# A graph network on one core: receiver's term moved into the message, messages two chunks ahead, deviation in two halves

## The reference, cut to what matters

```python
h = relu(layernorm(x))
m = concat(h[dst], h[src]) @ W_pre.T + b_pre            # one message per edge
mx, mn, s1, s2 = segment max, min, sum(m), sum(m*m) over dst   # 0 where a node has no edge
mean = s1 / deg_c;  std = sqrt(relu(s2 / deg_c - mean * mean) + 1e-5)   # deg_c = max(degree, 1)
agg = concat(mx, mn, mean, std)
scaled = concat(agg, agg * log(deg_c + 1), agg / log(deg_c + 1))
x = x + (concat(h, scaled) @ W_post.T + b_post) @ W_lin.T + b_lin

h = relu(layernorm(x))
agg = segment_sum(edge_attr, dst) / max(degree, 1)
x = x + relu(concat(h, agg) @ W1 + b1) @ W2 + b2
```

## Time and profile before

| | |
|---|---|
| median of 3 runs | 1519.05 us |
| profiled execution, own time | 1520.14 us |
| its span, first to last instruction | 1518.3 us |
| PE busy | 1445.0 us (95%) |
| DVE busy | 1287.0 us (85%) |
| POOL busy | 1152.0 us (76%) |
| ACT busy | 1142.2 us (75%) |
| mean granted TensorE clock | 0.979 of full |

### The profile page before, as it was taken

How to read it: one execution, slowest core, us unless ns; L and a number is a source line. 1 busy time by engine, 2 the same in 40 slices (tenths; PEclk the granted TensorE clock), 3 DMA queues, 4 the chain that set the end, 5 groups by cost and what they waited for, 6 DMA issues and landing times.

```text
span 1518.3 us, 34851 instructions
## 1 busy us (share of the span) xinstructions
PE 1445.0 (95%) x8704; PEld 1246.4 (82%) x8704; DVE 1287.0 (85%) x4128; ACT 1142.2 (75%) x2760; POOL 1152.0 (76%) x1427
## 2 busy tenths in 40 slices
PE   2799999999999987999999999999999999999994
PEld 2698998998998976888888888888888888888883
DVE  4899999999999957888888888888888888888881
ACT  1699999999999965777777777777777777777772
POOL 0677777777877876788888888888888888888722
PEclk9699999999999998999999999999999999999997
DMA  3455555555555563343434434333333443444200
GB/s 80 153 204 200 208 200 200 212 198 203 209 196 209 204 228 104 116 116 116 119 111 114 116 113 113 115 114 116 116 115 115 117 117 116 117 119 119 91 16 13
DMA packets 166068, 210.91 MB, mean 139 GB/s; under 512 B 19710, under 2 KB 116217, under 8 KB 166026
## 3 DMA queue, kind: packets, MB, share of 16 engines
q1 hardware_dynamic: 144074, 162.88, 32.7%
q0 software_dynamic: 21952, 47.55, 10.5%
HBM read 123.96 MB, written 90.27 MB: 141 GB/s over the span
## 4 chain that ended last, share of the span: by engine, by line
PE 92%; DVE 2%; issue 2%; DMA 1%; POOL 1%; ACT 1%; SPq 1%; DVEq 0%; POOLq 0%
PE bank L573 12%; PE bank L614 8%; PE bank L617 7%; PE bank L611 7%; PE bank L608 7%; PE bank L607 7%; PE bank L582 6%; PE bank L711 6%; PE bank L699 5%; PE bank L674 3%; PE bank L592 3%; PE bank L594 3%; PE bank L593 3%; PE bank L556 3%; PE bank L564 3%
## 5 line engine op out<-in xcount | busy, mean ns | idle before, releaser
L464 POOL DMA_INDIRECT y<-nout,oidx x196 | 223.3, 1139 | 49.0 <-issue 46.0
L456 POOL DMA_INDIRECT rows<-table,idx x196 | 187.9, 958 | 59.7 <-issue 59.7
L607 PE MATMUL bank<-comb_lo,agg_hi 128*128 128x384 f32 x588 | 221.3, 376 | 0.8 <-ACT bank L885 0.8
L456 POOL DMA_INDIRECT hs<-table,idx x196 | 192.8, 984 | 29.4 <-issue 10.0
L385 POOL TENSOR_TENSOR runs<-nx,b_all 128x512 f32<-128x512 f32 x98 | 125.5, 1281 | 114.6 <-DVE nx L1081 114.6
L573 PE MATMUL bank<-w_sb,nut 128*128 128x128 f32 x1568 | 202.0, 282 | 1.5 <-ACT nut L806 1.5
L573 PEld LDWEIGHTS bank<-w_sb,nut 128*128 128x128 f32 x1568 | 183.9, 193 | 19.8 <-issue 10.0
L611 PE MATMUL bank<-comb_hi,agg_lo 128*128 128x384 f32 x588 | 198.2, 337 | 0.0
L608 PE MATMUL bank<-comb_hi,agg_hi 128*128 128x384 f32 x588 | 198.1, 337 | 0.0
L791 ACT ACTIVATE nh<-nx,nms,nrs 128x128 f32<-128x128 f32 x392 | 161.8, 483 | 1.1 <-DVE nms L1054 0.5
L614 PE MATMUL bank<-comb_sd,agg_sd 128*128 128x384 f32 x392 | 158.1, 485 | 0.0
(11 more groups left out here) (184 smaller groups left out, 4192.1 us busy)
## 6 DMA issues: line engine op xcount, KB each, us to landing
table<-rows SPq DMA_DIRECT2D x98, 512.0 KB, 2.7
rows<-in_x SPq DMA_DIRECT2D x98, 256.0 KB, 3.1
y<-nout SPq DMA_DIRECT2D x98, 256.0 KB, 2.7
inv<-inv_row SPq DMA_DIRECT2D x49, 256.0 KB, 5.0
keepm<-keepm_row SPq DMA_DIRECT2D x49, 256.0 KB, 5.8
attr<-in_edge_attr SPq DMA_DIRECT2D x48, 256.0 KB
keep<-keep_row SPq DMA_DIRECT2D x49, 128.0 KB, 3.6
reset<-reset_row SPq DMA_DIRECT2D x49, 128.0 KB, 4.6
```

The lines of the kernel that those rows point to most:

```text
L456: pool.indirect_dma_start(out=to[:, s, j, :], out_offset=None, in_=of, in_offset=bass.IndirectOffsetOnAxis(ap=idx[:, s, which, j:j + 1], a ...
L464: pool.indirect_dma_start(out=out, out_offset=bass.IndirectOffsetOnAxis(ap=oidx[:, c % 4, j:j + 1], axis=0), in_=eout[:, c % 2, j, :], in_ ...
L607: pe.matmul(acc[:, 0:SCALERS * P], hi, w_lo, start=False, stop=False, skip_group_check=True)
```

## The change

- **Message.** `sender_part` becomes `messages`: a second plain fp32 matmul adds the receiver's term (`wd_t`, `hdt`). `comb_h`, `hdl`, `receiver_low` and their three matmuls per tile in `layer0` go.
- **Table.** Its second half holds x1 of a node without edges (the first layer's result in the node passes) instead of x; the seed of the edge part is reduced by that node's constant. So the table store of chunk c leaves at SyncE's node step c instead of c-2 and waits for `n_x1`; x is loaded into a buffer of its own, and the norms wait for the table store of the chunk four before.
- **Two chunks ahead.** In step k, PE and ACT make the message of chunk k+2; DVE scans chunk k+1 as before, in another order.
- **Deviation.** It is split into `high_part` and `low_part` like the others; three fp32r matmuls replace the plain one.
- **POOL.** Its edge steps are written out (no loop), so that the index columns are read in place and the copies `idx` and `oidx` go; `copy_factors` moves to DVE. Small additions keep their place between the indirect DMAs.
- **Order.** DVE: `scan_attr(k)` moves from the head of the step to behind `mix(k, 1)` and the low part of the maximum. ACT: `scale_attr(k + 1)` moves from the middle to the head, in front of `squares(k - 1)` and `seed(k, 1)`. SyncE's `edge_step` is unchanged.

```diff
 # TensorE
-                for a in (MX, MN, ME):
+                for a in (MX, MN, ME, SD):
...
-                pe.matmul(acc[:, 0:SCALERS * P], agg_sd[:, c % 2, cols], comb_sd[:].rearrange("p s f -> p (s f)"),
-                          start=False, stop=False, skip_group_check=True)
-                for h, w in ((hdt, comb_h_lo), (hdl, comb_h_hi), (hdt, comb_h_hi)):
-                    mm = pe.matmul(acc[:, 0:SCALERS * P], h[:, c % 2, cols], w[:].rearrange("p s f -> p (s f)"),
...
-                pe.matmul(bank[3 + c % 2][:], ws_t[:], hst[:, c % 2, :], start=True, stop=True).then_inc(sem("e_b_psum"), 1)
+                pe.matmul(bank[3 + c % 2][:], ws_t[:], hst[:, c % 2, :], start=True, stop=False)
+                pe.wait_ge(sem("e_hdt"), c + 1 + EU * i)
+                pe.matmul(bank[3 + c % 2][:], wd_t[:], hdt[:, c % 2, :], start=False, stop=True).then_inc(sem("e_b_psum"), 1)
...
-                if ahead:
-                    turn_sender(k + 1, i)
-                    turn_receiver(k + 1, i)
                 if have:
                     turn_attr(k, i)
-                if ahead:
-                    sender_part(k + 1, i)
+                if edge(k + 2):
+                    turn_sender(k + 2, i)
+                    turn_receiver(k + 2, i)
                 if have:
-                    pe.wait_ge(sem("e_hdl"), k + 1 + EU * i)
                     layer0(k, 0, i)
                     layer0(k, 1, i)
+                if edge(k + 2):
+                    messages(k + 2, i)
                 if behind:
-                    turn_normed(k - 1, i, not ahead)
+                    turn_normed(k - 1, i, not edge(k + 2))
 # ScalarE, edge_step
                 if ahead:
-                    sender_turned(k + 1, i)
+                    scale_attr(k + 1, i)
+                if behind:
+                    squares(k - 1, i)
                 if have:
                     seed(k, 1, i)
                 if behind:
-                    squares(k - 1, i)
                     spread(k - 1, i)
-                if ahead:
-                    message_squared(k + 1, i)
+                if edge(k + 2):
+                    receiver_turned(k + 2, i)
+                    sender_turned(k + 2, i)
                 if behind:
                     normalise(k - 1, i)
                 if have:
                     seed(k, 2, i)
+                if ahead:
+                    mean_squared(k + 1, i)
                 if behind:
                     normed_turned(k - 1, i)
...
 # SyncE, node_step
-                c = k + 2
+                c = k
                 if node(c):
...
+                    sp.wait_ge(sem("n_x1"), c + 1 + NU * i)
 # GpSimd
-            run_passes(pool, node_step, edge_step)
+            run_passes(pool, node_step, edge_step, edge_loop=False)
```

More of the change, by code:

```diff
@@ L236, in run_passes @@
                 edge_step(k - N_HI + 1, 0)
+        if not edge_loop:
+            for k in range(0, E_HI):
+                edge_step(k, 0)
+            return
         for k in range(0, E_LOOP):
@@ L399, in node_step, with go, column, gather_tile @@
                     last.then_inc(sem("n_norm1_pool"), 1)
[L401 to L422, removed]
-                s = c % 4
-                pool.wait_ge(fixed, 1)
+            def go(n, c, name, count):
+                if name:
+                    pool.wait_ge(sem(name), count)
+                if c >= 1:
+                    pool.wait_ge(sem(f"e_paused{n}"), c)
+                pool.tensor_tensor(pause_go[:, n:n + 1], eps_col[:], eps_col[:], ALU.add).then_inc(sem(f"e_paused{n}"), 1)
+            def column(which, c, j):
+                return index[:, which, 2 * c + j // 2, j % 2:j % 2 + 1]
+            def gather_tile(c, j):
+                s = c % 4
+                for which, to, of in ((0, hs, table_halves), (1, rows, table)):
+                    pool.indirect_dma_start(
+                        out=to[:, s, j, :], out_offset=None, in_=of,
+                        in_offset=bass.IndirectOffsetOnAxis(ap=column(which, c, j), axis=0)).then_inc(sem(f"e_gathered{s}"), 16)
+            def gather(c):
+                s = c % 4
                 if c == 0:
@@ L450, in gather @@
-            def gather(c, tiles, i):
-                s = c % 4
-                for j in tiles:
-                    if j % 2 == 1:
-                        pause(j // 2, c, i)
-                    for which, to, of in ((0, hs, table_halves), (1, rows, table)):
-                        pool.indirect_dma_start(
-                            out=to[:, s, j, :], out_offset=None, in_=of,
-                            in_offset=bass.IndirectOffsetOnAxis(ap=idx[:, s, which, j:j + 1], axis=0)).then_inc(sem(f"e_gathered{s}"), 16)
@@ L526, in _ @@
             pe.wait_ge(sem("part_sum_ready"), 1)
-            for s in range(SCALERS):
-                to = bank[5][:, s * P:(s + 1) * P]
-                mm = pe.matmul(to, w_pre_sb[:, 0:P], part_sum[:, s, :], start=True, stop=(s > 0))
-                if s == 0:
-                    mm = pe.matmul(to, w_post_sb[:, 0:P], w_lin_t[:], start=False, stop=True)
-            mm.then_inc(sem("comb_h_psum"), 1)
             pe.wait_ge(sem("comb_copied"), 1)
@@ L692, in hidden @@
                     pe.wait_ge(sem("e_out"), c + EU * i)
-                if m == 1 and edge(c + 2):
-                    pe.wait_ge(sem("e_hdl"), c + 3 + EU * i)
+                if m == 1 and edge(c + 3):
+                    pe.wait_ge(sem("e_hdt"), c + 4 + EU * i)
                 if c >= 1:
@@ L753, in _ @@
             for s, a, block_psum in comb_blocks:
-                to = comb_sd[:, s, :] if a == SD else comb_hi[:, a, s, :]
-                last = act.activation(to, block_psum, ACT.Copy)
+                last = act.activation(comb_hi[:, a, s, :], block_psum, ACT.Copy)
+                if a == SD:
+                    last = act.activation(comb_sd[:, s, :], block_psum, ACT.Copy)
             last.then_inc(sem("comb_copied"), 1)
@@ L937, in edge_step @@
                 if ahead:
[L938 removed]
+                    high_part(SD, "e_std", var[:], k + 1, i)
                 if behind:
                     out_bias(k - 1, i)
[L941 to L942 removed]
+                if edge(k + 2):
+                    message_squared(k + 2, i)
                 if behind:
@@ L1301, in edge_step @@
                 have, ahead, behind = edge(k), edge(k + 1), edge(k - 1)
-                if have:
-                    scan_attr(k, i)
+                if ahead:
+                    scan_max(k + 1, i)
+                    scan_squares(k + 1, i)
+                    scan_sum(k + 1, i)
                 if edge(k - 2):
@@ L1307, in edge_step @@
                     factors(k - 1, i)
+                if ahead:
+                    message_mean(k + 1, i)
                 if have:
```

213 lines of the change are left out of this document (104 added, 109 removed).

## The result

| | kernel before | changed kernel |
|---|---|---|
| median | 1519.09 us | 1655.14 us (1653.55 to 1665.76, 4 runs) |
| profiled execution | 1520.14 us | 1665.76 us |
| its span | 1518.3 us | 1664.0 us |

The ratio is 1.0904, 95% interval 1.0862 to 1.0946: slower by 9%. The forecast was 1695 us with a range of 1595 to 1775. The profiled execution is the longest of the four runs, 11 us above their median; the prediction's sum, 1696, is to be held against it.

A forecast was written before the change was run, and what follows sets the result against it. PE bounds the edge loop before; after the change, a ring through the late attribute load. 1520.14 + 175 (ring with half clock) - 7 + 8 = 1696, so 1695 us; own range 1640 to 1750, 8 in 10 1595 to 1775.

The forecast's parts named there:

- The ring: Edge loop: attribute landing, `scale_attr` through `scan_attr`, masks, next attribute load; 20.8 us a step, 45 steps, +103 us.
- L, the landing: Time from the attribute load's issue on SyncE to its landing, a term of the ring: 6.1 us, bounds 5.3 and 7.1.
- The clock: PE at half speed after idling 4.0 us before `layer0(k,1)`: 3.2 us lost, every second step, +1.6 per step.
- no drop: Rival: dense work beside PE's idle keeps the clock up in the edge loop; 1624 us; chance 0.17.
- a drop in every step: Rival: PE's clock drops in each of 45 edge steps, 24.0 us a step, +247, 1768 us; chance 0.17.
- Start and tail: Start of the edge part +8 us, first gather near 558; the four steps outside the ring gain 7 us.
- All of these fit by their sums, and I cost them at nothing: DVE about 15.9, ACT 14.2, POOL between 15 and 18.5 us per edge step against PE's 16.81; cost 0.
- PE's sum decides, up to 1500 if POOL holds it near 18: Rival: edge step of 16.81 us, order misread; 1443 us, or up to 1500; chance 0.06.
- The removed matmuls: PE's edge step: 2.60 us removed from `layer0`, 0.86 added for messages; 1.74 us less per step, 85 us if alone.

The follow-up runs named there:

- e4: Kernel before with only the order moves: `scale_attr` then `squares` ahead of the seed, `scan_attr` behind `mix(k, 1)`; 1587.66 us, ratio 1.0445.
- e1: Changed kernel with SyncE issuing the attribute load of chunk k+2 ahead of the masks' waits; 1487.71 us, ratio 0.9788.
- e2: Changed kernel with ACT's `scale_attr(k + 1)` moved back from the head to behind `normed_turned`; 1500.69 us, ratio 0.9872.
- e7: Changed kernel with `scan_attr(k)` back at the head of VectorE's step; 1489.45 us, ratio 0.9817.
- e8: e1 without GpSimd's six small additions per step; 1432.32 us, ratio 0.9435 to the kernel before.
- e5: Changed kernel plus ten plain fp32 matmuls of 128 columns ahead of `layer0` of tile 1, steps 1 to 45; 1608.21 us, ratio 1.059.
- e6: Changed kernel with the attribute load issued third, behind two masks, the other three behind it; 1563.44 us, ratio 1.0301.
- e9: Changed kernel, attribute load directly ahead of the five masks, behind the same waits; 1617.53 us beside 1655.32 for the kernel before.
- e11: The kernel of e9 run again; 1681.82 us beside 1740.14 for the kernel before, ratio 0.9661.

## Why the prediction was right, and where its sizes were off

- **The ring.** Right: its members, its place, its effect on each engine, and that 45 steps pay it. e4 makes it from the kernel before, e1, e2 and e7 each undo it. Its sum was right too: with the landing as measured it is 20.84 - 0.7 = 20.14, and the six steps at full clock took 20.14 us on the mean.
- **L, the landing.** The term that was mis-sized most: 5.4 us instead of 6.1. keepm's load, on which I had based it, lands 5.3 us after its issue in the changed kernel instead of 5.8, and the attributes land 0.57 + 5.4 - 5.3 = 0.7 us behind it instead of 0.86. L is 45 x 0.7 = 31 us, about the distance between the sum of 1696 and the profiled 1665.8. PE's idle time was shorter for it, 3.1 instead of 4.0 us.
- **The clock.** The mean was near, 1.7 us per step against 1.6, by two errors that cancel, and that is luck: half clock came in 39 of 45 steps, not in every second one, and cost 2.0 us in each, not 3.2. The rival "no drop" is refuted. The rival "a drop in every step" had nearly the right count, but its price of 3.2 us is reached nearly by the sixteen slowest steps alone (3.0 us above the six, the other 23 by 1.3): it would give 24.0 us a step and 1768 us. The Trainium skill's rule (TensorE: Matmul & The Clock Gate, "HAM oscillation"), that PE comes back at half clock each time anew, agrees with 39 of the 45 steps here and not with the other six, whose idle stretches were as long. What decides between them no run here shows.
- **Start and tail.** The start +10.7 instead of +8 (the first gather left at 558.38; I had said near 558). The steps outside the ring -3.9 (step 0) and -8.1 (from step 46 to the end) instead of -7 for all four.
- **"All of these fit by their sums, and I cost them at nothing".** True only under the ring's cover, and wrong for GpSimd without it: 17.9 us per step with the pauses between its indirect DMAs against PE's 16.8. In the changed kernel this is hidden; once the ring is open it is 45 x (17.97 - 16.71) = 57 us, about the measured difference of e1 and e8 (55). The prediction knew of the pauses and named 18 us as possible in a rival, but didn't price them. The rival "PE's sum decides, up to 1500 if POOL holds it near 18" is what e1 (1488) and e8 (1432) show; its 1443 was 11 us too high.
- **The removed matmuls.** The gain of 1.74 us per step is real: it is 18.55 - 16.71 = 1.84 between the kernel before and e8.

## What to carry to other kernels

When a change moves a consumer earlier and its producer's trigger later, follow the trigger through every queue on the way, and write the circle down with its length: if it passes a queue on which other loads stand ahead, the place of one load can outweigh what the engines save (here 167 us against 85). Before costing an engine at nothing by its busy sum, add its pauses: for GpSimd with indirect DMAs they were 0.15 to 0.30 us each, twelve to a step. And once one bound is open, read the next one off before stopping: the load first gave 2%, the small additions another 3.7%.

## What the runs showed of the hardware

- A plain fp32 matmul of 128 columns was followed by the next after 0.22 us (24 in 5.3), a transpose of the same tile after 0.11.
- A broadcast mask load of 128 KB at the head of SyncE's queue lands after 3.5 us; 256 KB of attributes at its head land after 3.1 (least 2.9), behind two masks after 5.6, behind five after 5.4 to 5.8 by the kernel (changed kernel 5.4, e5 5.7, e4 5.8).
- With PE idle for 3.1 us per step on the mean, half clock came in 39 of 45 steps of the changed kernel, and idle stretches of the same length went without it in six. With the idle time cut to 1.2 us (36.2 / 31, e5) it came in 3 of 45, and in e6 three steps had it beside idle stretches of only 1.8 us.
- A GpSimd addition of one column took 0.20 us at least and 0.21 in the median in e1's edge loop, but up to 1.2 (218 of them).
- On the chips of two jobs single edge steps took up to 33 us (traces of e9 and e11), with waits of up to 15.8 us that the trace puts down to nothing on the core ("issue", "remote"); why was not found out.
